# ScalarE's order in the dense slot of a two-layer graph network: where the store of the middle block and the load of the next table's number are issued

## The reference

```
h = relu(layernorm(x))                      # 6250 nodes x 256
for l in range(2):
    weights = softmax(z @ envW[l] + envb[l])            # 4 experts
    agg     = mean of z[src] over the edges into a node # 106250 edges
    outputs = concat([agg, z]) @ W[l][k] + z            # k = 0..3
    z       = relu(sum_k weights[:, k] * outputs[:, k])
return x + z
```

## Time and profile before

| | us |
|---|---|
| median of 3 runs | 1683.12 (1680.87 to 1683.23) |
| the profiled execution, its device time | 1683.16 |
| the span of its trace | 1681.3 |
| TensorE matmuls, busy | 1540.1 (92%) |
| TensorE weight loads, busy | 1108.8 (66%) |
| ScalarE, busy | 570.7 (34%) |
| VectorE, busy | 881.8 (52%) |
| GpSimd, busy | 1223.3 (73%) |

### The profile page before, as it was taken

How to read it: one execution, slowest core, us unless ns; L and a number is a source line. 1 busy time by engine, 2 the same in 40 slices (tenths; PEclk the granted TensorE clock), 3 DMA queues, 4 the chain that set the end, 5 groups by cost and what they waited for, 6 DMA issues and landing times. The chain is left out here.

```text
span 1681.3 us, 35043 instructions
## 1 busy us (share of the span) xinstructions
PE 1540.1 (92%) x8488; PEld 1108.8 (66%) x8489; DVE 881.8 (52%) x2024; ACT 570.7 (34%) x1247; POOL 1223.3 (73%) x1187
## 2 busy tenths in 40 slices
PE   1149999999999999999996499999999999999998
PEld 1027777666777776677773377777777777777775
DVE  7755566667666665666663134444433444444444
ACT  5323444444344344444430022222222222222221
POOL 2277777777777777777774677777777777777776
PEclk9999999999999999999997699999999999999999
DMA  9677777777777777767779978777777777787776
GB/s 282 233 226 213 219 219 214 218 218 208 215 218 219 217 225 216 216 197 222 220 211 349 347 241 243 238 236 243 238 238 228 234 246 240 239 245 238 239 240 201
DMA packets 157766, 393.09 MB, mean 234 GB/s; under 512 B 36717, under 2 KB 60808, under 8 KB 157732
## 3 DMA queue, kind: packets, MB, share of 16 engines
q0 software_dynamic: 92544, 302.70, 60.9%
q10 hardware_dynamic: 33576, 62.88, 10.2%
q1 hardware_dynamic: 31612, 27.07, 5.3%
HBM read 347.20 MB, written 45.37 MB: 233 GB/s over the span
## 5 line engine op out<-in xcount | busy, mean ns | idle before, releaser
L739 POOL DMA_INDIRECT ring<-zp_dram,gather_idx x1152 | 1202.7, 1044 | 386.9 <-issue 268.2
L1447 PE MATMUL agg_ps<-zp,stage 128*128 128x258 f32 x1568 | 455.8, 327 | 5.9 <-PEq L102 5.8
L1479 PE MATMUL mix_ps<-w_sb,turned_z 128*128 128x512 f32 x784 | 400.6, 611 | 8.2 <-PEq L102 8.2
L1479 PE MATMUL mix_ps<-w_sb,turned_m 128*128 128x512 f32 x784 | 390.5, 598 | 5.3 <-PEq L102 5.3
L1449 PE MATMUL agg_ps<-zp,stage 128*128 128x256 f32 x1568 | 387.4, 282 | 0.0
L1408 PE MATMUL agg_ps<-ring,onehot 128*128 x1248 | 378.7, 335 | 7.2 <-PEq L102 7.2
L1121 ACT ACTIVATE stage<-counts_sb 128x512 fp32r<-128x512 uint8 (+1 forms) x416 | 248.7, 605 | 395.9 <-ACTq L102 394.2
L1447 PEld LDWEIGHTS agg_ps<-zp,stage 128*128 128x128 f32 x1568 | 298.1, 190 | 62.8 <-issue 60.7
L1449 PEld LDWEIGHTS agg_ps<-zp,stage 128*128 128x128 f32 x1568 | 298.4, 190 | 37.9 <-issue 37.9
L1413 PE MATMUL agg_ps<-ring,onehot 128*128 x1248 | 318.0, 284 | 0.0
L1408 PEld LDWEIGHTS agg_ps<-ring,onehot 128*128 128x128 f32 x1248 | 239.4, 192 | 43.4 <-issue 42.2
(11 more groups left out here) (154 smaller groups left out, 883.4 us busy)
## 6 DMA issues: line engine op xcount, KB each, us to landing
ring<-zp_dram,gather_idx POOLq DMA_INDIRECT x1152, 3.8
zp_dram<-zp SPq DMA_DIRECT2D x7, 1792.0 KB, 7.9
a_dram<-counts_sb ACTq DMA_DIRECT2D x16, 784.0 KB, 5.0
zp_dram<-parts ACTq DMA_DIRECT2D x49, 256.0 KB, 2.7
counts_sb<-a_dram ACTq DMA_DIRECT2D x16, 784.0 KB
zp<-zp_dram ACTq DMA_DIRECT2D x4, 1792.0 KB, 21.8
parts<-in_x ACTq DMA_DIRECT2D x48, 128.0 KB
out_x<-z_out ACTq DMA_DIRECT2D x48, 128.0 KB
```

The costliest lines, as they stand in the source:

```text
L739: pool.indirect_dma_start(out=ring[:, k, t, 0:2 * D].bitcast(F32), out_offset=None, in_=zp_dram[l], in_offset=bass.IndirectOffsetOnAxis(ap ...
L1447: pe.matmul(agg_ps[:, bank, 0:D + 2], stage[:, g % 2, i, :], zp[:, c, D:2 * D + 2], start=c == 0, stop=True, skip_group_check=True)
L1479: mm = pe.matmul(mix_ps[i][:, :], (turned_z, turned_m)[what][:, c, :], w[:, i * HALF:(i + 1) * HALF], start=what == 0 and c == 0, stop=wha ...
```

## The change

In ScalarE's dense slot two things move. In both layers the load of the next table's number goes from behind the fill of group 9 to the slot's end. In the loop of layer 0 the store of the earlier block goes from behind the same fill to behind the copy of the transposed z. The first dense slot of a layer has no such store, and layer 1 has its own store earlier in the slot, where it stays.

```
                         if l:
                             free_result()
-                        for g in range(8, 10):
+                        for g in range(8, STAGES):
                             fill_stage(g)
-                        act.reg_mov(table_next, dense_no(act, r + 1))
+                        copy_z()
                         if prev is not None and l == 0:
                             finish(l, prev)
-                        for g in range(10, STAGES):
-                            fill_stage(g)
-                        copy_z()
                         begin(l)
+                        act.reg_mov(table_next, dense_no(act, r + 1))
```

## The result

The changed kernel took 1688.06 us in the median of 6 runs (1685.92 to 1691.28), the kernel before 1681.41 beside it (6 runs, 1680.67 to 1683.23): a ratio of 1.0036, 95% interval 1.0025 to 1.0047, slower by 0.25 to 0.47%. The prediction had 1685.6, with "the same" as the likeliest case.

The account below looks back on a forecast made before the run. TensorE, busy 92% of the span, was taken to bound the kernel. A gain of 5.4 us at group 10 and a loss of 7.9 at pair 2 gave +2.5 us on 1683.1, so 1685.6, range 1681.0 to 1688.0.

Parts of the forecast that it names:

- The end moves by what TensorE gains or loses: Whole kernel: TensorE, busy 92% of the span, sets the end through its gains or losses between matmuls, nothing else.
- Hence the store alone makes the gap, and the load ... costs nothing there.: Layer 0's loop, TensorE ahead of table group 10: the store alone causes the 0.36 us loss, the load none.
- rival D: Old place, layer 0: moving the store frees nothing, as the fill waits for something else; +7.9 us, 1691.0; chance 0.05.
- The gain, 15 x 0.36 = 5.4: Table group 10, layer 0's loop: the gap closes, saving 0.36 us in each of 15 rounds, 5.4 us.
- The store under the long wait, no cost: Behind the copy of z: the 0.34 us issue fits ScalarE's 5.15 us wait and lands before `z_out`; no cost.
- The load in layer 1, no cost: Slot's end in layer 1: ScalarE is idle 5.86 us before its next work, so zero in all 16 slots.
- The load behind `z_out`: Layer 0's slot end: 0.63 us of sequencer time delays pair 0's move; TensorE stalls 0.55 at pair 2, 14 times, 7.7.
- later in the slot nothing is added: Layer 0, behind the stall at pair 2: pair 3's own room of about 0.1 us absorbs the rest; no further loss.
- The entry, 0.2: Entry into layer 0's loop: more room ahead of pair 2, so TensorE stalls only 0.2 us, once.
- A: Load behind `z_out`: fully hidden by sequencer overlap, leaving only the 5.4 us gain, 1677.7; chance 0.09.
- B: Load behind `z_out`: half hidden, stalls of 0.24 us and none at the entry; -2.0 us, 1681.1; chance 0.11.
- C: Load behind `z_out`: takes 0.70 us instead of 0.28, as VectorE's loads do; +8.8 us, 1691.9; chance 0.07.

Follow-up runs that it names:

- first and third comparison: The changed kernel against the kernel before, measured two separate times: 1688.06 against 1681.41 us, and 1687.32 against 1682.78 us.
- three kernels that should agree: Against the kernel before: store alone moved, 1677.18 us; store and load moved, load ahead of `z_out`, 1676.94; load alone moved, ahead of `z_out`, 1676.68.

## Why the prediction was right and wrong, step by step

**The end moves by what TensorE gains or loses.** Right. The loop's stretch carried the sign in all eight comparisons. In the five of the other kernels it also has the size to within 0.8 us; for the changed kernel it is 3.7 of 6.65, 2.9 of 3.9 and 2.8 of 4.5, and the entry adds about 1 (below). What is left in the first and third comparison lies outside the loop and is most likely scatter.

**"Hence the store alone makes the gap, and the load ... costs nothing there."** Wrong, though the sum didn't depend on it. The control that I read it from, the first dense slot, has a load and no store; it shows that the load alone is covered, not that the store alone is exposed. The load used up the cover that the store would have had. The missing control was a slot with the store and without the load, which the trace of before doesn't hold; the kernel with the load alone supplied it. The rival D, "the store's move frees nothing", fell with the store alone.

**The gain, 15 x 0.36 = 5.4.** That the gap would go with the store was right, though the load's going would have closed it as well, and the term was too small. The loop of the store-only kernel is 0.46 per turn shorter. The missing 0.1 stood in the earlier trace rows: behind a gap the first matmul of a group is 0.2 ahead of the second (337.14 to 337.33), where it is 0.12 in a group that runs on. A gap costs its length and this 0.08, so 0.44 in that round, and the gap was somewhat longer in others. 15 x 0.46 = 6.9.

**The store under the long wait, no cost.** Right: `z_out` waits for 5.15 us as before in the changed kernel's trace.

**The load in layer 1, no cost.** Right: in the changed kernel's trace the 14 turns of layer 1 between the first table matmuls of its second and last dense slot take 619.3 us, before 619.2; the other seven traces lie between 618.9 and 619.9.

**The load behind `z_out`.** The sequencer's 0.63 was measured as 0.65 (1.29 less 0.64), the stall at pair 2 as 0.56 where 0.55 stood in the prediction, and it is there in all 14 turns. But "later in the slot nothing is added" was wrong by 0.09 per turn: behind pair 3 TensorE's sequencer takes its semaphore late, and the branch and the register operations ahead of the gathered unit then come late too. I had checked only whether pair 3's own matmul would be late. 14 x 0.65 = 9.1, not 7.7. From pair 1 to pair 4 the 14 turns together take 9.1 to 9.6 longer in the three changed traces than before.

**The entry, 0.2.** Mis-sized. Pair 2 stands 1.31 behind the matmuls ahead of it in the changed trace, before 0.86 (153.18 to 154.04), another 0.28 follows at the gathered unit (0.13 behind pair 3 before, 0.41 now) and another 0.29 from there to the products of `turned_m` (0.60 and 0.89), so 1.0 in all. From pair 1 to pair 4 it is 4.03 before and 5.05, 5.06 and 4.92 in the three changed traces. TensorE before, then changed:

```profile
155.12 0.38 PE L1460 MATMUL win_ps<-win_key,win_lo 128*128 128x245 bf16 x2
155.25 0.37 PE L1408 MATMUL agg_ps<-ring,onehot 128*128 x1
155.85 0.67 PE L1479 MATMUL mix_ps<-w_sb,turned_m 128*128 128x512 f32 x1
```

```profile
154.14 0.38 PE L1458 MATMUL win_ps<-win_key,win_lo 128*128 128x245 bf16 x2
154.55 0.38 PE L1406 MATMUL agg_ps<-ring,onehot 128*128 x1
155.44 1.10 PE L1477 MATMUL mix_ps<-w_sb,turned_m 128*128 128x512 f32 x2
```

The timeline of the changed kernel shows that the move starts 1.26 behind `z_out` here, against 0.38 before; I had put in 0.63 as inside the loop, and it was 0.88. TensorE at pair 2 and ScalarE at the move, in the changed trace:

```profile
151.75 1.02 PE L1477 MATMUL mix_ps<-w_sb,turned_z 128*128 128x512 f32 x2
153.06 0.37 PE L1458 MATMUL win_ps<-win_key,win_lo 128*128 128x245 bf16 x2 [0.28 <-PEq L102]
```

```profile
150.81 0.42 ACT L1189 ACTIVATE z_out<-mix 128x256 f32<-128x256 f32 x1 [5.05 <-ACTq L102]
152.07 0.58 ACT L1135 ACTIVATE counts_sb<-win_ps 128x490 uint8<-128x490 f32 x1 [0.85 <-ACTq L102]
```

**The sum.** With the measured terms: -6.9 + 9.1 + 1.0 = +3.2, near the +2.5 on record, because a gain too small by 1.5 and a loss too small by 2.2 us mostly cancelled. That the sum came out close is luck. So it is with a single turn: it got 0.20 to 0.26 longer, where 0.55 - 0.36 = 0.19 was forecast, because both terms were too small by 0.1. The three comparisons gave +6.65, +3.9 and +4.5. The 1688.06 of the first lies 0.06 over the top of the range, the other two medians inside it. The likeliest case was put as "the same", and the kernel is slower by 0.2% to 0.36%; the forecast's centre, 0.15%, lay close to that line, and with a bound of 3.4 us the chance of 0.25 for slower was low. The rivals A, B and C are out: the load lasted 285 ns, and the move of pair 0 came later by the whole 0.65.

The Trainium skill, "DMA: Bandwidth & Descriptors", section "Rules for kernel authors", wants a DMA issued early; here the later issue cost nothing, since the landing fitted into the wait of 5.15 us, and it gained nothing over the early one once the load was out of its way (loops of 671.1 and 671.0). So no run here speaks against the rule. The figure of about 600 ns for a `tensor_load`, in the same page's section "Latency and other measured facts", was not met by the 285 ns measured at the new place.

## What to carry to other kernels

Work of a sequencer (a register load, a DMA issue) cost nothing here where its engine had an instruction of about the same length running (0.63 us of load under a fill of 0.63), where a wait of 5 us was ahead, or where nobody waited for what came behind it (the load in layer 1). Two such items behind one instruction share a single cover, so test each alone before one is blamed. Where another engine waits for the next result, place them ahead of the instruction that ends a long wait and not behind it: here these are two neighbouring lines, and swapping them is worth some 10 us of 1687. A busy share of 34% says nothing about that.

## What the runs showed of the hardware that was not expected

- A load of one number from SBUF into a ScalarE register lasts 0.28 us, but with its address, its check and its move it holds the sequencer for 0.63 to 0.65 (`z_out` to the move: 0.64 without, 1.29 with, 1.83 with two, the second of which has one register operation fewer).
- A stalled group of table matmuls pays 0.08 us beyond its wait, since its first two matmuls start 0.19 to 0.20 apart and not 0.12. The stalled window pair doesn't: its two start 0.11 apart, as before.
- Issuing one of the stores of line 1194 held ScalarE's sequencer for 0.34 to 0.38 us in the loops of all nine traces. Between the layers, where other transfers are issued around it, single ones took 2.5, 4.1, 5.8 and 6.7 us in four of the nine traces. That stretch, from the sixteenth dense slot of layer 0 to the second of layer 1, took 150.4 to 154.8.
- The end took 56.3 to 60.0 us in three traces of the same changed kernel, and 55.7 to 60.0 in all nine. The 14 turns of the loop agree to 0.1 us among three kernels that should agree, and to 0.9 among the three traces of the changed one.
